# Attention heads with four query quarters in the column groups of TensorE, values of two tiles at a time, results kept on chip

## The reference

```
qkv = h @ w_qkv + b_qkv                      # h: [4, 1024, 256]
q, k, v = ...                                # 8 heads of 32
scores = einsum('bnhd,bmhd->bhnm', q, k) / sqrt(32)
attn = softmax(scores, axis=-1)
vals = einsum('bhnm,bmhd->bnhd', attn, v)
out = vals @ w_proj + b_proj
```

## Time and profile before

| | |
|---|---|
| median of 3 runs | 1323.39 us (1320.49 to 1324.12) |
| the profiled execution | 1324.85 us, span of the trace 1323.0 us |
| PE busy | 1219.5 us (92%) |
| DVE busy | 682.5 us (52%) |
| ACT busy | 420.2 us (32%) |
| mean granted clock of TensorE | 0.95 of full speed |
| heads, 356 to 909 us | 552.8 us |

### The profile page before, as it was taken

The page is one execution under the profiler, slowest core; times in us unless marked ns, Lnnn a source line. Parts: engine busy times, 40 slices in busy tenths (PEclk is TensorE's granted clock), DMA queues, the critical chain, the costliest instruction groups (busy, mean ns, idle before and its releaser), DMA issues. The chain is left out here.

```text
span 1323.0 us, 21162 instructions
## 1 busy us (share of the span) xinstructions
PE 1219.5 (92%) x6723; PEld 772.7 (58%) x6724; DVE 682.5 (52%) x1540; ACT 420.2 (32%) x465; POOL 207.6 (16%) x418
## 2 busy tenths in 40 slices
PE   6899999895999999999999999998971999999995
PEld 3677676663534444444443444434861899999995
DVE  3265455446666666666666666652862333333331
ACT  1312132220255555555555555553210111111110
POOL 0002030302000000000000000000054244434442
PEclk8899999795999999999999999998965999999998
DMA  6203353131532332323323322205636565656551
GB/s 196 56 2 118 132 171 128 64 127 64 201 102 53 90 83 76 96 64 96 93 63 90 83 55 64 64 9 158 216 140 159 169 207 188 210 185 211 194 199 64
DMA packets 97141, 156.78 MB, mean 119 GB/s; under 512 B 44848, under 2 KB 65264, under 8 KB 96464
## 3 DMA queue, kind: packets, MB, share of 16 engines
q1 hardware_dynamic: 86576, 121.81, 30.1%
q0 software_dynamic: 9712, 31.35, 7.4%
q10 hardware_dynamic: 816, 3.15, 0.7%
HBM read 108.77 MB, written 44.06 MB: 116 GB/s over the span
## 5 line engine op out<-in xcount | busy, mean ns | idle before, releaser
L215 DVE TENSOR_REDUCE s_nmax<-h_ps_m 128x1 f32<-128x512 f32 x488 | 314.4, 686 | 178.2 <-PE h_ps_m L209 177.7
L928 ACT ACTIVATE h_expd<-h_ps_e 128x1024 f32<-128x1024 f32 x256 | 261.9, 1024 | 237.4 <-PE h_ps_e L946 232.6
L962 PE MATMUL h_ps_o<-h_expd,h_ones 128*32 128x512 f32 x1024 | 270.7, 604 | 0.0
L962 PE MATMUL h_ps_o<-h_expd,s_vh 128*32 128x512 f32 x1024 | 270.7, 604 | 0.0
L1559 PEld LDWEIGHTS ps_h<-xs_c,lnt 128*128 128x128 f32 x1248 | 148.2, 195 | 4.8 <-issue 2.9
L1559 PE MATMUL ps_h<-xs_c,lnt 128*128 128x128 f32 x1248 | 148.6, 278 | 2.3 <-DVE xs_c L1511 2.3
L1569 PE MATMUL ps_y<-w,vals_t 128*128 x624 | 141.2, 379 | 0.6 <-DVE ys L1524 0.6
L578 PE MATMUL a_ps_v<-a_val,a_expd 128*128 128x257 f32 x512 | 120.0, 388 | 5.1 <-ACT a_expd L456 4.5
L1569 PEld LDWEIGHTS ps_y<-w,vals_t 128*128 128x128 f32 x624 | 115.5, 190 | 15.1 <-issue 1.0
L1600 ACT ACTIVATE vals_t<-ps_h 128x1024 f32<-128x1024 f32 x39 | 39.9, 1024 | 263.3 <-DVE ps_h L1504 263.3
L1504 DVE TENSOR_TENSOR ps_h<-ps_h,b_t 128x1024 f32<-128x1024 f32 x39 | 48.1, 1233 | 131.5 <-PE ps_h L1559 131.5
(11 more groups left out here) (188 smaller groups left out, 1421.9 us busy)
## 6 DMA issues: line engine op xcount, KB each, us to landing
lnt<-in_w SPq DMA_DIRECT2D x39, 1024.0 KB, 4.8
qk_scr<-a_head_hi SPq DMA_DIRECT2D x16, 512.0 KB, 2.7
qk_scr<-a_head_lo SPq DMA_DIRECT2D x16, 512.0 KB, 3.6
w<-in_w POOLq DMA_DIRECT2D x8, 1024.0 KB, 6.1
xs<-xs_scr SPq DMA_DIRECT2D x39, 128.5 KB, 2.0
a_x_t<-in_x_t POOLq DMA_DIRECT2D x4, 1024.0 KB, 10.4
r_scr<-a_res POOLq DMA_DIRECT2D x4, 1024.0 KB, 6.0
v_scr<-res SPq DMA_DIRECT2D x4, 1024.0 KB, 3.9
```

What stands on the lines that cost most here:

```text
L215: self.nc.vector.tensor_reduce(self.nmax[k][:, nb, half:half + 1], ps_m[:, half, :], AX.X, ALU.max, negate=True).then_inc(self.v_max, 1)
L928: nc.scalar.activation(expd[:, m % RING, :], flat(ps_e[m % 2]), ACT.Exp, scale=SCALE).then_inc(a_exp, 1)
L962: mm = nc.tensor.matmul(ps_o[k][c:c + D, :], w, expd[:, m % RING, half * HALF:(half + 1) * HALF], start=(m == 0), stop=(m == NB - 1))
```

## The change

The four column groups now hold four quarters of the queries. Per tile there are four products of 256 columns with v, one for each quarter, and then a second round of four with ones, which puts the denominators beside the values in the same bank, already at the place of the values they divide. So the turn of the sums and their copy are gone; DVE takes the reciprocal of 128x256 and multiplies. Four DMAs put a head's results, channels on rows, in the SBUF tile `vals`, which the output stage projects from directly. PE's order is now by pairs: scores, maxima, scores, maxima, and then the values of two tiles. `expd` has room for 8 tiles instead of 4. The lead of the maxima is 14 blocks, the two more being put into the end of `conv_phase`. The weights `w2` of the experts are loaded by SP in the loop of heads, in a layout prepared on the host, and no longer by POOL.

```diff
-LEAD = NB + NB // 2
+LEAD = 2 * NB - 2
-        HEAD_BLOCKS = (2, 2, 2, 1, 1, 1, 1, 1, 1)
+        HEAD_BLOCKS = (2, 2, 2, 2, 2, 1, 1, 1, 1)
@@ head_phase, SP
-                    sp.dma_start(io["o_scr"][bass.ds(t + j // HG, 1), :, :, j % HG * D:(j % HG + 1) * D].rearrange("o p j d -> p (o j) d"),
-                                 outh[j % 2][:, :, :]).then_inc(out_stored[j % 2], 16)
+                    sp.wait_ge(v_norm, SLOTS * t + j + 2)
+                    for q in range(4):
+                        sp.dma_start(vals[j * D:(j + 1) * D, bass.ds(t, 1), q * QUARTER:(q + 1) * QUARTER].rearrange("p o c -> p (o c)"),
+                                     outh[j % 2][q * D:(q + 1) * D, :]).then_inc(out_stored[j % 2], 16)
@@ head_phase, ACT
-                        nc.scalar.activation(expd[:, m % RING, :], flat(ps_e[m % 2]), ACT.Exp, scale=SCALE).then_inc(a_exp, 1)
-                        if m == 1 and not first:
-                            outputs(t, j - 1)
+                        nc.scalar.activation(expd[:, m, :], flat(ps_e[m % 2]), ACT.Exp, scale=SCALE).then_inc(a_exp, 1)
+                        if m == 2 and left >= 1:
+                            hd.next_rows(act, ps_o[j % 2], t, j + 1)
@@ head_phase, PE
-                def values(s, k, m):
-                    for half in range(2):
-                        for kind, w in enumerate((vh[s][:, m, :], ones[:, :])):
-                            c = (2 * half + kind) * D
-                            mm = nc.tensor.matmul(ps_o[k][c:c + D, :], w, expd[:, m % RING, half * HALF:(half + 1) * HALF],
-                                                  start=(m == 0), stop=(m == NB - 1))
+                def values(j, m):
+                    for q in range(4):
+                        nc.tensor.matmul(ps_o[j % 2][q * D:(q + 1) * D, 0:QUARTER], vh[j % SLOTS][:, m, :],
+                                         expd[:, m, q * QUARTER:(q + 1) * QUARTER], start=(m == 0), stop=(m == NB - 1))
+                    for q in range(4):
+                        last = nc.tensor.matmul(ps_o[j % 2][q * D:(q + 1) * D, QUARTER:2 * QUARTER], ones[:, :],
+                                                expd[:, m, q * QUARTER:(q + 1) * QUARTER], start=False, stop=(m == NB - 1),
+                                                skip_group_check=True)
+                def head(t, j, first=False, left=SLOTS):
+                    h = SLOTS * t + j
+                    for c in range(NB // 2):
+                        for i in (2 * c, 2 * c + 1):
+                            if i == 0:
+                                pe.wait_ge(*hd.loaded(maxrow_in, 32, t, j))
+                            if not (first and i < 2):
+                                pe.wait_ge(a_exp, NB * h + i - 1)
+                            scores(j % SLOTS, i)
+                            ahead = 1 if i < 2 else 2
+                            if left >= ahead:
+                                ...
+                                hd.maxima(pe, ps_m, NB * h + LEAD + i, (j + ahead) % SLOTS, (i + LEAD) % NB)
+                        if c == 0:
+                            if not first:
+                                tail(j - 1)
+                                pe.wait_ge(v_norm, h)
+                            if left >= 1:
+                                hd.max_turn(pe, ps_o[j % 2], ident, t, j + 1)
+                        else:
+                            ...
+                            for m in (2 * c - 2, 2 * c - 1):
+                                values(j, m)
@@ head_phase, DVE
+                def norm(t, j):
+                    h, got = SLOTS * t + j, ps_o[j % 2]
+                    dve.wait_ge(pe_pv, NB * (h + 1))
+                    dve.wait_ge(v_norm, h + 1)
+                    nc.vector.reciprocal(rc[:, :], got[:, QUARTER:2 * QUARTER]).then_inc(v_rc, 1)
+                    dve.wait_ge(v_rc, h + 1)
+                    dve.wait_ge(out_stored[j % 2], 16 + 64 * (SLOTS // 2 * t + j // 2))
+                    nc.vector.tensor_tensor(outh[j % 2][:, :], got[:, 0:QUARTER], rc[:, :], ALU.mult).then_inc(v_norm, 1)
...
+                        if i == 1 and left >= 1:
+                            hd.split_max(dve, t, j + 1)
+                        if i == 2 and not first:
+                            norm(t, j - 1)
```

More of the change, by code:

```diff
@@ L45 @@
 REGION = TB * P + P
+QUARTER = N // 4
 STACK = 3 * D
@@ new lines, in tail @@
+                def tail(j):
+                    for m in range(NB - 2, NB):
+                        values(j, m)
[10 more added lines that the diff above has]
+                            if left >= ahead:
+                                if i == 2:
+                                    if first:
+                                        pe.wait_ge(g_set, SLOTS - EARLY)
+                                    pe.wait_ge(*hd.loaded(stack_in, 16 * STACK_DMAS, t, j + 2))
+                                hd.maxima(pe, ps_m, NB * h + LEAD + i, (j + ahead) % SLOTS, (i + LEAD) % NB)
+                        if c == 0:
+                            if not first:
+                                tail(j - 1)
+                                pe.wait_ge(v_norm, h)
+                            if left >= 1:
+                                hd.max_turn(pe, ps_o[j % 2], ident, t, j + 1)
+                        else:
+                            if c == 1:
+                                if first:
+                                    pe.wait_ge(out_stored[0], 16)
+                                if left >= 1:
+                                    pe.wait_ge(hd.a_mrow, h + 2)
+                            for m in (2 * c - 2, 2 * c - 1):
+                                values(j, m)
@@ new lines, in _ @@
+                stream(pe, head)
+                pe.wait_ge(a_exp, NB * HEADS)
+                tail(SLOTS - 1)
+            @block.vector
+            def _(dve):
+                nc.vector.memset(rc[:, :], 0.0).then_inc(v_norm, 1)
+                def norm(t, j):
[6 more added lines that the diff above has]
+                    nc.vector.tensor_tensor(outh[j % 2][:, :], got[:, 0:QUARTER], rc[:, :], ALU.mult).then_inc(v_norm, 1)
@@ L968, in head @@
                     for i in range(NB):
[L969 to L975, removed]
-                        if left >= ahead:
[L977 to L980, removed]
-                            hd.maxima(pe, ps_m, NB * h + LEAD + i, (j + ahead) % SLOTS, (i + NB // 2) % NB)
@@ L1078, in output_phase @@
         v_onehot, pe_count = sem("v_onehot", "pe_count")
[L1079 to L1081 removed]
+        consts_in, res_in = sems["consts_in"], [sems[f"res_in{k}"] for k in range(2)]
+        pe_pr, pe_l2t, pe_rt, a_l2t = sem("pe_pr", "pe_l2t", "pe_rt", "a_l2t")
         v_step, v_res1, v_l2, v_rt = sem("v_step", "v_res1", "v_l2", "v_rt")
@@ L1311, in expert_phase @@
                   for k in range(2)]
-        hid_t = [keep["vals_t"][:, k, :, :] for k in range(2)]
+        hid_t = [keep["vals"][:, k, :].rearrange("p (k n) -> p k n", n=P) for k in range(2)]
         ys = sb("ys", [P, C])
```

140 lines of the change are left out of this document (27 added, 113 removed).

## The result

The changed kernel takes 1378.12 us (median of 4 runs, 1376.93 to 1379.52), the kernel before in the same session 1323.76: a ratio of 1.0415 [1.0393, 1.0436]. The profiled execution has a span of 1376.5 us against 1323.0. The forecast was 1376, within 1350 to 1402.

What follows compares the result with a forecast made beforehand. PE was taken to bound the heads' stage, busy 551 of 553 us. Terms of +44 for that stage, +9 for the convolution's tail and -1 for the output stage sum to +52, about 1376 us, range 1350 to 1402.

Steps and rivals of the forecast that it cites:

- The pair's lead: Scores, maxima, scores, maxima before a pair's values: S to V 2.77 us, of which 0.71 is waiting for DVE's reductions.
- Two tiles of values: Values of a pair: 1.85 us plus 0.02 for 256-column passes, one emptying of 0.13 saved.
- the rival that had them at 1430: Short 256-column value passes starve on loads, a pair grows by 0.44 us, the kernel takes 1430; chance 0.13.
- The reciprocal: Division on DVE, one reciprocal of 128x256 per head: 1.87 us, at 6.7 ns an element.
- The stall behind it: Third pair's maxima wait for their bank because of DVE's division: 0.35 to 0.37 us a head.
- The threshold of 1.5 us: Division on DVE: with a reciprocal under 1.5 us no stall follows it, 11 us less, 1365.
- Head 0: First head of the stage: +2.3 us on 15.7 before.
- Heads without maxima: Last two heads: a pair takes 3.0 us, saving some 3 us.
- The convolution's tail: Two more blocks of maxima there wait for DVE: +7.5 us for both, taken as +9 with the lower clock.
- one sign of being wrong that came true: The forecast would be wrong if the granted clock fell below 1.00 in the heads.
- The output stage: No load of values, turn or copy, but three more store issues: -1 us, bounds -5 and +4.
- The sum: Whole kernel: 44 + 9 - 1 = +52 us, about 1376.

Runs made afterwards that it cites:

- e2_thin: The changed kernel with DVE reducing only 64 of the 512 columns of each half of the maxima in the heads; 1295.01 us, ratio 0.9788.
- e8_mssm_halves: The changed kernel with pairs ordered maxima, scores, scores, maxima, and the reciprocal in two 128-column halves after blocks 3 and 5; 1327.31 us, ratio 1.0023.
- e9_half_ones: The changed kernel with the round of ones left out for every second tile; 1339.62 us, ratio 1.0129.
- e5_recip2: The changed kernel with each head's reciprocal done twice, the first result unread; 1445.01 us, ratio 1.0918.
- e10_load: The changed kernel with the third stack's six loads issued ahead of the ones, three on ACT's queue; 1379.61 us, ratio 1.0414.
- e3_blocks: The changed kernel with the list of maxima blocks per head altered to (3, 3, 2, 1, 1, 1, 1, 1, 1); 1370.72 us, ratio 1.0341.
- e4_warm: The changed kernel with unused transposes on PE in the output stage, 40 behind the second projection group, 16 behind each of the next two; 1372.12 us.

## Why the prediction was right, step by step

**The pair's lead.** Forecast 2.77 for S to V, measured 2.79; the loader's 117.4 us behind `s_nmax` against some 110. The step was read from an order with the same shapes that stood at one place of the old trace. e2_thin shows its cause: with reductions of 64 columns the same order takes 2.05, and 2.06 was the forecast without a wait.

**Two tiles of values.** Forecast 1.87, measured 1.86 (702.89 to 704.75). The four-group passes of 256 columns do not starve; the rival that had them at 1430 is out. e9_half_ones shows that they are on the path.

**The reciprocal.** Forecast 1.87, measured 1.75. With e8_mssm_halves' 0.95 for 128 columns it is (1.75 - 0.95) / 128 = 6.2 ns an element; the strided slope of 6.7 was too high. The 2.13 that I had worked out from the Trainium skill ("VectorE: DVE Perf Modes", the 8-slice walkthrough) is further off, and the measurement decides.

**The stall behind it, 0.37 a head: wrong.** It was 0. The length is only part of that: block 3 was reduced from 713.74 on, 4.31 behind the second pair's S (709.43), where I had 4.70. Of the 0.39, 0.12 are the shorter reciprocal; it also starts 0.16 earlier (711.62, where I had 2.35 behind S), and the reduction starts 0.08 before the product's end. The working itself stands: with 4.31 put in, its V comes at 7.37, before the 7.41 of a pair without a stall. The second M of the third pair then gets its banks at 715.80 and 716.40, 1.75 and 2.35 behind its S (714.05), as in any pair (1.76 and 2.35). The threshold of 1.5 us, under which the stall was to go, was too low by at least 0.25; e5_recip2 and e9_half_ones show that there is hardly more slack than what was used. So a head is 18.62, not 18.96, and the 29 heads gave 36 instead of 45.

**Head 0: too small.** Forecast +2.3, measured +6.4 (15.7 to 22.1). I had left out that a lead of 14 asks for the third stack within the first pairs of head 0, while its loads are only issued when the stage begins. PE waits for it in the middle of the head (2.46 of idle loader, in the section on e10_load), and its products on both sides of the wait run at the lower clock: the rounds of values from 376.35 on are 0.86 and 0.61 apart instead of 0.46 and 0.43. The head in the table of stretches:

```profile
366.00:388.00 22.00, 18.48 (x129) 9.64 (x129) 11.09 (x20) 8.16 (x9) 3.20 (x5) 0.77 0.62 185
```

This is the one sign of being wrong that came true: the granted clock of the heads was to stay at 1.00 and is 0.99, and all of that lies in head 0; from 388 on it is 1.00 in every stretch.

**Heads without maxima.** Pairs of 3.0 were forecast and are there; about -2.3 instead of -3.

**The convolution's tail.** Forecast +9, measured +10.1. Two idle stretches of the loader of 3.1 us each, and projections of 5.29 and 6.08 us behind them instead of 3.60, were the two parts that I had priced, but not in these shares. From the maxima behind a projection to the next projection it is now 3.8 and 4.0 us longer (forecast 7.5 for both), the two projections behind the waits take 1.7 and 2.5 longer at the lower clock (forecast 1.5 for both), and the first projection starts 1.5 earlier (326.07, before 327.52), which no term had: the closeness is in part luck. e3_blocks removes both waits.

**The output stage: wrong sign.** Forecast -1, measured +3.9. I had counted the freed time of DVE, not what PE's freed time does. With the turns in it PE was busy for 46.3 us of 50 (920 to 970 before) at 1.00; without them it idles for 5.1 us ahead of 980.68, and the clock is 0.82 over 970 to 1010. With work put in, e4_warm measures -1.0 against before. That this is the forecast's own number is chance, since the forecast had no such work in it.

**The sum.** 36 + 6.4 - 2.3 + 10.1 + 3.9 = 54, against 52. The total is closer than its parts: 9 us too much for 29 heads stand against 4 too few for head 0, 5 for the output stage and 1 for the tail. So the nearness of the total is in part luck. What holds by its own rows is the wait of 0.7 us in a pair, the length of the values, and the two waits in the tail.

## What to carry to other kernels

When work is put in pairs, look at what each half of the pair waits for from the one before: a wait of 0.7 us that another step had hidden cost 2.9 us a head, more than the pairing (1.4) and the removed transposes (0.4) gave, and moving one of two blocks to the front of the pair got two thirds of it back in a plain pair (4.65 to 4.18, 3.95 without a wait). A slow engine-side operation (here a division) is best cut where that engine idles, and its slack is to be measured with the order as it will be, not as it was. Work that is taken off a busy TensorE does not only free time: where it leaves the engine idle, the products behind it can run at the lower clock, as they did in the output stage here (0.82, and 1.00 with the work put back).

## What was not expected of the hardware

The granted clock fell behind a 1.86 us wait of TensorE's loader in some heads of e5_recip2 and not in others with the same rows ahead, at 1.2 to 2.8 us a head. Adding 72 unneeded transposes to the output stage shortened it by 4.9 us. Six loads of 128 KB, issued 1.4 us behind a store of 1 MB and from two queues, took 4.7 to 5.0 us to land; issued from 2.9 us behind it on and from one queue they took 2.6 to 3.1.
